# Attention's scores made a second time, transposed: no transposes of the probabilities, values in float32

## The reference

```python
h = _layernorm(x, axis=-1) * (1 + ca) + sa
# 16 heads of 16 channels; Q, K, V are h (normalised once more) times weights plus biases
scores = jnp.einsum('bhqd,bhkd->bhqk', Q, K) / jnp.sqrt(jnp.float32(D_HEAD))
scores = jnp.where(causal, scores, jnp.float32(-jnp.inf))
A = jax.nn.softmax(scores, axis=-1)
AV = jnp.einsum('bhqk,bhkd->bhqd', A, V)
x = x + ga * (AV.reshape(x.shape) @ Wo + bo)
```

## Time and profile before

| | |
|---|---|
| median of three runs | 1127.13 us (1124.58 to 1129.17) |
| the profiled execution | its span is 1155.7 us; no other time of it is given, so the span stands for it, 28.6 us over the median |
| attention's inputs | 0 to 94.9 us |
| attention, first score to last copy of `O` | 94.9 to 343.7 us |
| attention's output, shared expert, sorting | 343.7 to about 540 us |
| busy shares of the whole span | PE 83%, DVE 65%, ACT 57%, POOL 40% |

### The profile page before, as it was taken

How to read it: one execution, slowest core, us unless ns; L and a number is a source line. 1 busy time by engine, 2 the same in 40 slices (tenths; PEclk the granted TensorE clock), 3 DMA queues, 4 the chain that set the end, 5 groups by cost and what they waited for, 6 DMA issues and landing times. The chain is left out here.

```text
span 1155.7 us, 21305 instructions
## 1 busy us (share of the span) xinstructions
PE 957.4 (83%) x5505; PEld 801.8 (69%) x5505; DVE 746.7 (65%) x1932; ACT 657.2 (57%) x1705; POOL 458.8 (40%) x641
## 2 busy tenths in 40 slices
PE   6678799999978744687999994078989998999994
PEld 2466688888866633465899994056867777888883
DVE  4885799999974753338755552799746777444453
ACT  3568889999972333327766663367853334433331
POOL 3477556666640566501344443457620111200000
PEclk8788999999997766798999997589989998999997
DMA  7067844444404422307543434730032232102012
GB/s 250 13 210 178 216 108 91 91 91 92 91 8 138 154 75 91 133 14 253 188 129 121 130 121 151 257 116 1 12 104 70 87 108 76 47 28 65 28 56 87
DMA packets 109867, 123.53 MB, mean 107 GB/s; under 512 B 44192, under 2 KB 82848, under 8 KB 109656
## 3 DMA queue, kind: packets, MB, share of 16 engines
q1 hardware_dynamic: 101128, 99.19, 30.5%
q0 software_dynamic: 8656, 23.33, 5.5%
HBM read 77.87 MB, written 44.62 MB: 106 GB/s over the span
## 5 line engine op out<-in xcount | busy, mean ns | idle before, releaser
L746 ACT ACTIVATE PR<-PS,nmax 128x128 f32<-128x128 f32 (+3 forms) x256 | 135.6, 551 | 12.6 <-DVE nmax L786 11.2
L663 POOL TENSOR_SCALAR PR<-PR,rinv 128x128 f32<-128x128 f32 (+3 forms) x256 | 132.3, 536 | 0.0
L786 DVE TENSOR_REDUCE nmax<-PS 128x1 f32<-128x128 f32 (+3 forms) x256 | 113.7, 481 | 20.2 <-PE PS L689 14.8
L1384 POOL DMA_INDIRECT r_results<-r_y,r_to x79 | 76.0, 963 | 112.8 <-DVE r_to L1439 76.6
L794 DVE TENSOR_TENSOR PTlo<-PS,PThi 128x512 fp32r<-128x512 f32 (+1 forms) x192 | 103.1, 590 | 2.9 <-ACT PThi L756 2.9
L756 ACT ACTIVATE PThi<-PS 128x512 fp32r<-128x512 f32 (+1 forms) x192 | 96.7, 545 | 6.1 <-PE PS L701 6.0
L688 PE MATMUL PS<-K,Q 128*128 128x128 f32 (+3 forms) x256 | 83.4, 385 | 12.0 <-DMA Q<-q_parts 8.9
L701 PE MATMUL PS<-ident,PR 128*128 128x128 f32 x640 | 85.8, 279 | 3.2 <-DVE PTlo L794 2.6
L717 PE MATMUL PS<-PThi,V 128*128 128x512 f32 (+3 forms) x256 | 85.1, 345 | 1.0 <-DVE PTlo L794 0.5
L2511 DVE TENSOR_TENSOR H<-PS,H 128x256 f32<-128x256 f32 x72 | 30.6, 424 | 81.9 <-ACT H L2472 80.2
L2472 ACT ACTIVATE H<-PS 128x256 f32<-128x256 f32 x72 | 27.6, 385 | 97.2 <-PE PS L2631 96.1
(11 more groups left out here) (393 smaller groups left out, 3099.5 us busy)
## 6 DMA issues: line engine op xcount, KB each, us to landing
r_xg<-r_sorted SPq DMA_DIRECT2D x79, 129.0 KB
r_wst<-in_routed SPq DMA_DIRECT2D x16, 608.0 KB
K<-k_parts SPq DMA_DIRECT2D x64, 128.0 KB
Q<-q_parts SPq DMA_DIRECT2D x32, 128.0 KB
Q<-q_parts SPq DMA_DIRECT2D x64, 64.0 KB
V<-v_parts SPq DMA_DIRECT2D x64, 64.0 KB, 2.4
mlp_st<-r_results SPq DMA_DIRECT2D x8, 512.0 KB, 7.2
c_yg<-r_results SPq DMA_DIRECT2D x8, 512.0 KB, 8.3
```

Of the source, the lines that this page charges most:

```text
L663: pool.tensor_scalar(PR[:, e % 4, i, 0:w], PR[:, e % 4, i, 0:w], rinv[:, e % 4, i:i + 1], 1.0, ALU.mult, ALU.mult).then_inc(norm_done, 1)
L746: act.activation(PR[:, e % 4, i, 0:w], k.PS[:, i, 0:w], ACT.Exp, bias=nmax[:, e % 4, i:i + 1], accum_out=rsum[:, e % 4, i:i + 1]).then_inc ...
L786: dve.tensor_reduce(nmax[:, e % 4, i:i + 1], k.PS[:, i, 0:P * (i + 1)], AX_X, ALU.max, negate=True).then_inc(max_done, 1)
L1384: pool.indirect_dma_start(out=d.results, out_offset=bass.IndirectOffsetOnAxis(ap=to[:, i % TO_LANES:i % TO_LANES + 1], axis=0), in_=y[:, i ...
```

## The change

Attention goes by pairs x of heads, 32 of them. Scores are still made with queries on partitions, but only for their maxima: PE makes two heads from Q on 96 rows (48 a head: three products of high and low parts), DVE takes the maxima of both heads in one instruction. The negated maxima, high and low, are transposed by PE (`shift_rows`), copied by ACT to `mrow`, and SP brings them by four DMAs into four more rows of `Q`, against rows of ones in `K`. Then PE makes the scores a second time with keys on partitions (`columns`, 100 rows, K times Q), which has the maxima subtracted already; DVE takes the minimum with `cap` in place in PSUM on the diagonal 128x128 blocks, which masks them; ACT's exponential writes the transposed probabilities to `PT` in float32, five units of 512 columns a pair. `values` are float32 matmuls, one a head and key tile, from 32 columns of `V` (16 of V, 16 of ones, which give the sums) into 32 partitions of `O`. `O` is transposed back and divided by DVE (`normalize`), gathered in `A`, and transposed once a batch to `OT`, now with 128 full rows: two tiles of 128 for the output product in place of four. V stays in SBUF; the splits of V, POOL's scaling, ACT's and DVE's `hi` and `lo`, and the ten transposes a head are gone. POOL's `fill` stands where `zero` stood. A pair's stages run at lags of 0 (scores, maxima), 1 (shift), 2 (columns, cuts, exponentials), 4 (values), 5 and 6 steps.

```diff
+KQ_LANES = 3
+ROWS = 3 * DH
+SHIFT = 2 * ROWS
+PAIRS = B * QUADS * 2
+S_ORDER = (3, 0, 2, 1)
+CHUNK_AT = (0, 4 * P, 8 * P, 7 * P)
+KEY_UNITS = ((0, (0,)), (1, (0,)), (0, (1, 3)), (1, (1, 3)), (None, (2,)))
...
+    def fill(self, pool):
+        ones = slice(SHIFT, P)
+        pool.memset(self.V[:].rearrange("p b t h e -> p (b t h) e")[:, :, DH:2 * DH], 1.0).then_inc(self.filled, 1)
+        for u in range(KQ_LANES):
+            pool.memset(f32(self.K[u][:]), 0.0).then_inc(self.filled, 1)
+        pool.memset(self.cap[:], -MASKED).then_inc(self.filled, 1)
+        pool.wait_ge(self.filled, KQ_LANES + 2)
+        pool.affine_select(out=self.cap[:], in_=self.cap[:], compare_op=ALU.is_ge, fill=MASKED,
+                           base=0, pattern=[[1, P]], channel_multiplier=-1).then_inc(self.filled, 1)
+        pool.wait_ge(self.filled, KQ_LANES + 3)
+        for u in range(KQ_LANES):
+            pool.memset(f32(self.K[u][ones]), 1.0).then_inc(self.filled, 1)
+        pool.wait_ge(self.filled, 2 * KQ_LANES + 3)
+        for u in range(KQ_LANES):
+            for j in range(2):
+                own = self.K[u][ones, j:4:2, :]
+                pool.affine_select(out=own, in_=f32(own), compare_op=ALU.is_ge, fill=0.0,
+                                   base=-2 if j else 1, pattern=[[0, 2], [0, T]], channel_multiplier=1 if j else -1).then_inc(self.filled, 1)
+        pool.wait_ge(self.filled, self.FILLED)
...
+    def load(self, sp, n, halves=range(2)):
+        b, q, u = n // QUADS, n % QUADS, n % KQ_LANES
         for j in halves:
-            r, heads = 64 * j, slice(j, 4, 2)
-            src = self.k.k_parts[b, q, heads].rearrange("s a r t -> (a r) s t")
-            for dup in range(2):
-                sp.dma_start(f32(self.K4[u][r + 32 * dup:r + 32 * dup + 32, heads, :]), src).then_inc(self.k_in[u], 16)
-            src = self.k.q_parts[b, q, heads]
-            sp.dma_start(f32(self.Q4[u][r:r + 32]), src.rearrange("s a r t -> (a r) s t")).then_inc(self.q_in[u], 16)
-            for dup in range(2):
-                sp.dma_start(f32(self.Q4[u][r + 32 + 16 * dup:r + 48 + 16 * dup]),
-                             src[:, 1 - dup].rearrange("s r t -> r s t")).then_inc(self.q_in[u], 16)
-    def load_values(self, sp, b, q, u):
-        for s in range(4):
-            sp.dma_start(f32(self.V4[u][:, :, s, 32 * s:32 * s + 32]),
-                         self.k.v_parts[b].rearrange("t p h d -> p t h d")[:, :, q * 4 + s, :]).then_inc(self.v_in[u], 16)
+            r, heads = ROWS * j, slice(j, 4, 2)
+            keys, queries = self.k.k_parts[b, q, heads], self.k.q_parts[b, q, heads]
+            sp.dma_start(f32(self.K[u][r:r + 32, heads]), keys.rearrange("s a r t -> (a r) s t")).then_inc(self.kq_in[u], 16)
+            sp.dma_start(f32(self.K[u][r + 32:r + 48, heads]), keys[:, 0].rearrange("s r t -> r s t")).then_inc(self.kq_in[u], 16)
+            sp.dma_start(f32(self.Q[u][r:r + 16]), queries[:, 0].rearrange("s r t -> r s t")).then_inc(self.kq_in[u], 16)
+            sp.dma_start(f32(self.Q[u][r + 16:r + 48]), queries.rearrange("s a r t -> (a r) s t")).then_inc(self.kq_in[u], 16)
...
+            for x in range(PAIRS):
+                sp.wait_ge(m_copied, x + 1)
+                for t in range(TT):
+                    sp.dma_start(f32(Q[x // 2 % KQ_LANES][SHIFT:SHIFT + 4, x % 2, t * P:(t + 1) * P]), mrow[4 * t:4 * t + 4, x % 2, :]).then_inc(m_in[x % 2], 16)
+                n, half = x // 2 + 2, x % 2
+                if KQ_LANES <= n < PAIRS // 2:
+                    load(n, half)
...
+            def scores(u):
+                def stage(x):
+                    lane, p, i, unit = x // 2 % KQ_LANES, x % 2, S_ORDER[u], 4 * x + u
+                    if u == 0 and p == 0:
+                        pe.wait_ge(kq_in[lane], 128 * (x // 2 // KQ_LANES + 1))
+                    w = P * (i + 1)
+                    if unit >= 2:
+                        pe.wait_ge(max_done, unit - 1)
+                    for j in range(2):
+                        pe.matmul(S_BANK(u, j)[:, 0:w], Q[lane][0:SHIFT, p, P * i:P * i + P], K[lane][0:SHIFT, 2 * p + j, 0:w], start=True, stop=False)
+                    for j in range(2):
+                        last = pe.matmul(S_BANK(u, j)[:, w - P:w], k.identb[:], k.maskb[:], start=False, stop=True)
+                    last.then_inc(s_ready, 1)
+                return stage
+            def columns(v):
+                def stage(x):
+                    lane, p, unit = x // 2 % KQ_LANES, x % 2, len(KEY_UNITS) * x + v
+                    if v == 0:
+                        pe.wait_ge(m_in[x % 2], 64 * (x // 2 + 1))
+                    wait(pe, exp_done, unit - 1)
+                    own, tiles = KEY_UNITS[v]
+                    at, r = 0, slice(0, SHIFT + 4)
+                    for j in range(2) if own is None else (own,):
+                        for n in tiles:
+                            w = T - P * n
+                            last = pe.matmul(ST_BANK(unit)[:, at:at + w], K[lane][r, 2 * p + j, P * n:P * n + P], Q[lane][r, p, P * n:T], start=(at == 0), stop=(at + w == T))
+                            at += w
+                    last.then_inc(st_ready, 1)
+                return stage
...
+            def shift_rows(x):
+                pe.wait_ge(shift_done, x + 1)
+                wait_side("shift", x)
+                pe.transpose(SIDE[0:4 * TT, 0:P], f32(shift[:, x % 2].rearrange("p t j a -> p (t j a)")), k.ident[:]).then_inc(mT_ready, 1)
+            def values(half):
+                def stage(x):
+                    q = x // 2
+                    if x % 2 == 0 and half == 0:
+                        if q == 0:
+                            pe.wait_ge(heads.filled, heads.FILLED)
+                        pe.wait_ge(exp_done, 2 * len(KEY_UNITS) * (q + 1))
+                        wait(pe, o_copied, q)
+                    n = (0, 3, 1, 2)[2 * (x % 2) + half]
+                    w = T - P * n
+                    for s in range(4):
+                        last = pe.matmul(O[32 * s:32 * s + 32, P * n:T], V[:, q // QUADS, n, 4 * (q % QUADS) + s, :],
+                                         PT[:, q % 2, s, CHUNK_AT[n]:CHUNK_AT[n] + w], start=(n == 0), stop=(n == 2))
+                    if n == 2:
+                        last.then_inc(av_done, 1)
+                return stage
...
+            wavefront((0, scores(0)), (2, columns(0)), (5, quads(rows)), (2, columns(1)), (0, scores(1)), (4, values(0)), (2, columns(2)),
+                      (1, shift_rows), (0, scores(2)), (2, columns(3)), (4, values(1)), (6, batches(attended(0))), (2, columns(4)),
+                      (0, scores(3)), (6, batches(attended(1))), n=PAIRS)
...
+            def attended_row(q):
+                act.wait_ge(av_done, q + 1)
+                wait(act, oT_ready, q)
+                act.activation(osb[:], O, ACT.Copy).then_inc(o_copied, 1)
+            def exponential(v):
+                def stage(x):
+                    q, unit, (own, tiles) = x // 2, len(KEY_UNITS) * x + v, KEY_UNITS[v]
+                    act.wait_ge(cut_done, unit + 1)
+                    if x % 2 == 0 and v == 0:
+                        wait(act, av_done, q - 1)
+                    at, s = CHUNK_AT[tiles[0]], 2 * (x % 2)
+                    if own is None:
+                        w = T - P * tiles[0]
+                        out, src = PT[:, q % 2, s:s + 2, at:at + w], ST_BANK(unit)[:, 0:2 * w].rearrange("p (s w) -> p s w", s=2)
+                    else:
+                        out, src = PT[:, q % 2, s + own, at:at + T], ST_BANK(unit)
+                    act.activation(out, src, ACT.Exp).then_inc(exp_done, 1)
+                return stage
+            def shift_row(x):
+                act.wait_ge(mT_ready, x + 1)
+                if x >= 2:
+                    act.wait_ge(m_in[x % 2], 64 * (x // 2))
+                act.activation(mrow[:, x % 2, :], SIDE[0:4 * TT, 0:P], ACT.Copy).then_inc(m_copied, 1)
...
+            wavefront((2, exponential(0)), (2, exponential(1)), (2, exponential(2)), (1, shift_row), (2, exponential(3)), (6, batches(high(0))),
+                      (4, quads(attended_row)), (2, exponential(4)), (6, batches(high(1))), n=PAIRS)
...
+            def maximum(u):
+                def stage(x):
+                    i = S_ORDER[u]
+                    dve.wait_ge(s_ready, 4 * x + u + 1)
+                    dve.tensor_reduce(nmax[:, x % 2, i], k.PS[:, 2 * (u % 2):2 * (u % 2) + 2, 0:P * (i + 1)], AX_X, ALU.max,
+                                      negate=True).then_inc(max_done, 1)
+                return stage
+            def cut(v):
+                def stage(x):
+                    unit, tiles = len(KEY_UNITS) * x + v, KEY_UNITS[v][1]
+                    dve.wait_ge(st_ready, unit + 1)
+                    diagonal, cap = ST_BANK(unit)[:, 0:P], heads.cap[:]
+                    if tiles != (0,):
+                        far = 3 * P if tiles == (1, 3) else 2 * P
```

(103 more changed lines are left out.)

270 lines of the change are left out of this document (59 added, 211 removed).

## The result

The changed kernel takes 1197.53 us (median of three runs, 1195.06 to 1199.97) against 1126.39 us for the kernel before (1124.58 to 1129.17): a ratio of 1.063 (95% interval 1.0605 to 1.0659). A fourth run took 3406.64 us at a granted clock of 0.27, with which the median is 1198.75; all that follows goes without it. The change makes the kernel 71 us slower; +31 was forecast.

The account below looks back on a forecast made before the run. PE, DVE and ACT were taken as nearly full mid-attention; after the change a closed DMA loop of 8.1 us a step. Attention +26, POOL's fill +10, output -5: 1127 + 31 = 1158 us, 8-in-10 range 1112 to 1197.

Parts of the forecast that it names:

- +31: Whole kernel: 26 for attention, 10 for POOL's fill, -5 for the output, giving 1158 us.
- the loop through the DMA: Attention: each step's first columns wait for shift rows sent by four DMAs after the previous step's third exponential.
- The sum of the closed loop: Attention: PE 3.44, cut, exponential and copy to 4.77, then issues, landing and hand-overs: 8.1 us a step.
- first to fourth issue: SP: the fourth small DMA starts 3 x 0.40 = 1.2 us behind the first, read from two loads taking 0.80.
- the values: PE: four heads' float32 records take five places, 2.15 us for 512 columns, 1.61 for 384, 1.88 in the mean.
- rival A: Values on PE: four heads side by side, 6.97 us a step, 1118 us; gains below 7.12 a step; chance 0.27.
- B: Values on PE: heads run serially, 3.44 us for 512 columns, 9.23 us a step, 1195 us; chance 0.20.
- SP's list at the start: Start of attention: two steps of 3.3 us, with maxima and shifts alone, before the first columns.
- The output's 5 us: Output product: 12 of 24 matmuls a batch go, 0.43 us apart; the first batch on the path gives -5.
- POOL's fill: Before attention: the new fill takes 22.8 us against 7.0; net +10 (7 to 16) after what is given back.
- Rival C: DMA in attention: the four small transfers land in 3 us, each step 1 us longer, 1190 us; chance 0.08.
- Rival D: Attention: the loop isn't closed, DVE is the bound at 5.6 us a step, 1078 us; chance 0.05.

Follow-up runs that it names:

- e3: The changed kernel with twelve more matmuls a pair on PE, ahead of the last scores, filling its idle wait: 1166.95 us (1.036 of the kernel before).
- e6: The changed kernel with the four heads' values all summed into the same 32 rows of O, one behind another: 1252.4 us in one run.
- e5: The changed kernel with the first two pairs' shift-row transfers put ahead of the last batch's stores in SP's list: 1185.01 us (1.053).
- e1: The changed kernel with shift rows laid out by PE and copied by ACT straight into Q, no DMA transfer: 1114.14 us (0.989 of the kernel before).
- e7: The kernel before, unchanged, profiled again: 1124.2 us, span 1122.0.
- e4: The changed kernel with POOL's fill split between the start of its list and behind later roots: 1181.36 us (1.048 of the kernel before).
- e8: The kernel with the edits of e1 and e4 together (1100.71 us), with PT and V in bfloat16 instead of float32: 1109.7 us (0.986).

## Why the prediction was wrong

The mechanism was right: the loop through the DMA closes, sets the step (all but some 6 us of the 31 steps), and the work taken from DVE and ACT wins nothing. The direction was right too. The size was not. In the prediction's own terms:

| stretch | forecast | measured |
|---|---|---|
| first scores later | +10 | 106.88 - 94.9 = +12.0 |
| first scores to first columns | 2 x 3.3 = 6.6 | 130.56 - 106.88 = 23.7 |
| 31 steps | 31 x 8.1 = 251.1 | 31 x 8.67 = 268.7 |
| last first columns to the end of attention | 8.1 + 4 x 2.3 = 17.3 | 415.7 - 399.2 = 16.5 |
| behind attention | -5 | 777.7 - 778.1 = -0.4 |

The differences add up: 2.0 + 17.1 + 17.6 - 0.8 + 4.6 = 40.5 us over the +31, which makes 71.5, and the spans differ by 71.4. Three steps failed.

**The sum of the closed loop, 8.1 us.** Its terms against a step at full clock (e3) and one with the clock low (the changed kernel's, above):

| term | forecast | e3 | changed kernel |
|---|---|---|---|
| first columns to values | 0.46 + 0.3 + 0.40 = 1.16 | 1.41 | 1.70 |
| values | 1.88 | 1.00 | 1.44 |
| third columns to the cut | 0.40 | 0.54 | 0.83 |
| cut and exponential to the copy | 0.41 + 0.62 = 1.03 | 0.95 | 0.96 |
| copy and hand-over to SP | 0.3 + 0.1 | 0.28 | 0.28 |
| first to fourth issue | 1.2 | 2.50 - 0.58 = 1.92 | 1.92 |
| fourth issue to the next first columns (landing) | 2.0 | 1.65 | 1.79 |
| sum | 8.1 | 7.75 | 8.92 |

The step of e3 has four transposes of `rows` and a key tile of 512 columns (forecast 2.15), the changed kernel's has no `rows` and a tile of 384 (forecast 1.61). At full clock the loop is shorter than forecast: 7.75 and 7.1 by turns in e3, where the steps without `rows` are the shorter ones. What was left out is the clock: the prediction priced every PE term from the earlier trace rows at full clock and named a fall only as a thing that would make it wrong. But the loop itself makes the gap in which PE stands idle, and its length was forecast well: some 1.5 us a step, measured 26.9 us in the 18 steps from 160 to 320 us. The fall was part of the forecast's own mechanism. It costs 1 us a step, 31 us in all (e3). That 8.1 lies so near the 8.67 is in part luck: without the clock's part the step is 7.69, and the 31 x (8.1 - 7.69) = 13 us that the sum had too many hide as much of the clock's 31.

Of the other terms, the values were sized too long, 2.15 for a tile that takes 1.00: the four heads' records start together, two places and not five, so rival A was right on concurrency, and B's 3.44 us for 512 columns is what one group takes (e6, 3.55). The Trainium skill ("TensorE: Matmul & The Clock Gate", Part 3: Packing small matmuls) states 2.38 times for three groups; the traces agree, with 3.55 / 1.00 for four and float32. It didn't decide, since the issues took back most of that: 0.64 us apart instead of 0.40. That price was read from loads of K; a transfer of four partitions between two tiles costs SP more, in the earlier trace rows nothing showed it. Rival A's 6.97 would have been 7.1 and 7.75 by turns at full clock, in the mean above its own limit of 7.12, and with the clock as granted it was 8.67.

**SP's list at the start.** The prediction counted two steps of 3.3 us before the first columns and did not ask what stands in front of the first shift rows in SP's list. The last loads of a lane, the stores of the last batch and `wo`'s load do, 124.74 - 113.56 = 11.2 us. e5 and e1 start the first columns 10.4 and 13.6 us sooner.

**The output's 5 us.** From the end of attention to the first scatter it was 455.2 - 415.7 = 39.5 us against 385.3 - 343.9 = 41.4: 1.9 us won, and given back by the end. The term that failed is the 0.43 us for each of the 12 matmuls that go: in the kernel before (e7) only the first six of the 24 stand that far apart and nearly all others 0.23, while after the change it is nine of the 12. From attention's end to the first sum into `X` it became 10.0 us in place of 12.3.

**POOL's fill** was right: 26.99 to 47.82, 20.8 us for 22.8 forecast, net +12 for +10 (e4 takes that back). Rival C fell, with landings of 1.65 to 1.8 us. Rival D fell in this kernel, but it is what e1 makes of it: without the transfer the step goes to 6.1 to 6.25 us. That is above D's 5.6; what those steps rest on, the chain through the two banks of the transposed scores or VectorE's work, stays open. Only TensorE's passes for the values are ruled out (e8).

## What to carry to other kernels

When a change closes a loop between engines, price the loop with the clock that its own waiting leaves TensorE, not with the clock of the full engine before: here 1 us of 8.67 was that, and twelve matmuls a pair in the idle time brought it back. A transfer inside such a loop costs its issues one behind another plus its landing, here 1.92 + 1.8 us for 8 KB; four rows that TensorE can lay out and ScalarE can copy across partitions need no transfer at all (83.4 us less). And look along each queue at the first trip round, not only in the steady state: what stood ahead of the first small transfer, eight stores above all, cost about as much as the whole fill.
